# Attention block with a two-way expert layer on one core: the PV steps of a key chunk in one run of four, where they stood in two runs of two

## The reference

```
h = layernorm(x) * (1 + ca) + sa
x = x + ga * attention(h)          # 16 query heads, 4 key/value heads, head size 64, rotary, causal
h = layernorm(x) * (1 + cb) + sb
x = x + gb * experts(h)            # 8 experts (128 -> 512 -> 128, silu gate), top 2 of each token

logits = einsum('bqhgd,bkhd->bhgqk', q, k) / 8 ; masked above the diagonal
w = softmax(logits) ; out = einsum('bhgqk,bkhd->bqhgd', w, v) @ Wo + bo
```

## Time and profile before

| | |
|---|---|
| median of three runs | 1269.56 us |
| the profiled execution's own time | 1270.48 us |
| its span, first to last instruction | 1268.7 us |
| TensorE busy / VectorE busy | 86% / 67% of the span |
| ScalarE busy / GpSimd busy | 42% / 47% of the span |

### The profile page before, as it was taken

The page is one execution under the profiler, slowest core; times in us unless marked ns, Lnnn a source line. Parts: engine busy times, 40 slices in busy tenths (PEclk is TensorE's granted clock), DMA queues, the critical chain, the costliest instruction groups (busy, mean ns, idle before and its releaser), DMA issues.

```text
span 1268.7 us, 16442 instructions
## 1 busy us (share of the span) xinstructions
PE 1087.0 (86%) x5698; PEld 657.3 (52%) x5698; DVE 852.9 (67%) x1659; ACT 535.8 (42%) x1149; POOL 591.3 (47%) x639
## 2 busy tenths in 40 slices
PE   3589999999999999999999999999999840199930
PEld 2356555555555655455555555565555330199930
DVE  3657878776878786777878776878777374044422
ACT  1335544545445454544544545445444412144410
POOL 1725655634545673634645644544453336411136
PEclk9699999999999999999999999999999955599975
DMA  8000000000000000000000000000000061211112
GB/s 226 1 1 1 1 1 1 1 1 1 1 1 1 1 1 1 1 1 2 1 1 1 1 1 1 1 1 1 1 1 1 1 199 35 64 39 49 32 36 76
DMA packets 33088, 24.84 MB, mean 20 GB/s; under 512 B 8816, under 2 KB 28272, under 8 KB 33008
## 3 DMA queue, kind: packets, MB, share of 16 engines
q1 hardware_dynamic: 23664, 17.25, 4.5%
q0 software_dynamic: 2048, 4.20, 1.1%
q10 hardware_dynamic: 7296, 2.36, 0.8%
HBM read 15.54 MB, written 8.26 MB: 19 GB/s over the span
## 4 chain that ended last, share of the span: by engine, by line
PE 74%; DVE 11%; POOL 7%; issue 3%; DMA 2%; ACT 2%; ACTq 1%; POOLq 0%; DVEq 0%
PE PS L1156 19%; PE PS L1110 12%; PE PS L1138 11%; PE PS L1140 9%; PE PS L1221 4%; PE PS L1240 3%; POOL sent L586 3%; PE PS L1086 2%; PE PS L1175 2%; DVE part_max L847 2%; POOL full L600 2%; PE PS L1123 2%; PE PS L1093 2%; PE PS L1166 2%; DVE full L863 2%
## 5 line engine op out<-in xcount | busy, mean ns | idle before, releaser
L847 DVE TENSOR_REDUCE part_max<-PS 128x1 f32<-128x512 f32 (+2 forms) x576 | 340.1, 618 | 132.9 <-PE PS L1110 110.5
L656 ACT ACTIVATE full<-PS 128x512 f32<-128x512 f32 x384 | 223.4, 599 | 198.3 <-PE PS L1140 185.7
L1138 PE MATMUL PS<-rounded 128*128 128x512 f32 (+3 forms) x640 | 271.9, 425 | 5.9 <-ACT diag L665 2.4
L1110 PE MATMUL PS<-rounded 128*128 128x512 f32 (+3 forms) x640 | 250.0, 417 | 2.4 <-DVE V L828 1.3
L533 POOL TENSOR_TENSOR full<-full 128x512 f32<-128x512 f32 x128 | 164.0, 1313 | 156.2 <-PE PS L1156 155.2
L1140 PE MATMUL PS<-rounded 128*128 128x512 f32 (+3 forms) x640 | 233.3, 365 | 0.0
L665 ACT ACTIVATE diag<-PS 128x512 f32<-128x512 f32 (+3 forms) x256 | 111.3, 441 | 214.8 <-PE PS L1143 184.9
L1110 PEld LDWEIGHTS PS<-rounded 128*128 128x128 f32 x640 | 119.7, 193 | 138.2 <-DVE part_max L847 62.9
L561 POOL TENSOR_TENSOR rot_cos<-qkv_sb,cos_sb 128x320 f32<-128x320 f32 x64 | 60.4, 943 | 279.5 <-DVE qkv_sb L825 277.2
L1156 PE MATMUL PS<-full,V 128*64 128x512 f32 x768 | 190.0, 605 | 0.0
L1138 PEld LDWEIGHTS PS<-rounded 128*128 128x128 f32 x640 | 122.9, 192 | 80.8 <-ACT diag L665 27.0
(11 more groups left out here) (140 smaller groups left out, 1439.8 us busy)
## 6 DMA issues: line engine op xcount, KB each, us to landing
full<-in_L_ffn_experts_w_dram SPq DMA_DIRECT2D x16, 256.0 KB, 6.7
sent<-sum_cols SPq DMA_DIRECT2D x1, 2496.0 KB, 19.6
made<-attnT SPq DMA_DIRECT2D x39, 64.0 KB, 1.5
full<-sent SPq DMA_DIRECT2D x9, 256.0 KB, 3.0
out_dram<-XA SPq DMA_DIRECT2D x4, 256.0 KB, 2.4
wqkv<-in_L_attn_Wq_dram ACTq DMA_DIRECT2D x1, 512.0 KB, 4.3
bqkv<-in_L_attn_bq_dram ACTq DMA_DIRECT2D x1, 512.0 KB, 9.8
wo_sb<-in_L_attn_Wo_dram SPq DMA_DIRECT2D x1, 512.0 KB, 8.8
```

Of the source, the lines that this page charges most:

```text
L656: nc.scalar.activation(full[:, k % QUADS, r, :], PS[:, bank, :], ACT.Exp).then_inc(probs_ready, 1)
L847: nc.vector.reduce_max(part_max[:, t, b:b + 1], PS[:, bank, 0:width], AX.X).then_inc(ring_dve, 1)
L1110: last = nc.tensor.matmul(PS[:, bank, 0:w], QT[:, ch % 2, h, t * P:(t + 1) * P], KT[:, 0, keys:keys + w], start=True, stop=not last_bank)
L1138: nc.tensor.matmul(o, KT[:, 0, keys:keys + P], QT[:, ch % 2, h, q0:BANK], start=True, stop=False)
```

## The change

Off the diagonal the pending PV steps are now held until the scores of r = 3 are issued; before, they went out at r = 1 and r = 3. So behind the eight score steps of a key chunk come four PV steps in one run: the last one of the chunk before and tiles 0, 1 and 2. The room left on the line behind r = 0, 1 and 2 is 2.1 for each PV step that is pending by then (2.1, 4.2 and 6.3; before, 2.1 behind r = 0 and 2.1 behind r = 2), and the room of the run itself is 8.4 (before 4.2 twice). The `poolsum` of key chunk 1 in the stages with three key chunks off the diagonal moves from behind r = 1 to behind r = 3 of key chunk 2, since the PV step that it waits for is in that run. What is computed stays as it is.

```diff
             for r in range(TB):
                 main += [("s", J, q, r, 0), ("s", J, q, r, 1)]
-                if q < J // PAIRS and r % 2 == 0:
+                if q < J // PAIRS and r < TB - 1:
                     main.append(("gap", 2.1 * len(pending)))
                 else:
                     main += pending
                     pending = []
-                if r == (1 if q < J // PAIRS else 0) and q > 1:
+                if r == (TB - 1 if q < J // PAIRS else 0) and q > 1:
                     if q < CHUNKS - 1:
                         main += [("poolsum", J, m, q - 1) for m in range(2)]
                     else:
                         main += [("quadsum", J, m, part) for m in range(2) for part in range(4)]
                 pending.append(("pv", J, q, r))
```

## The result

The changed kernel takes 1292.1 us (median of 4 runs, 1291.3 to 1295.9) against 1269.4 us, a ratio of 1.0186 with a 95% interval of 1.0163 to 1.0208. The forecast was 1265.0 us, so the sign was wrong, and the time lies far above the 1275 up to which the wide range reached. The profiled execution took 1295.9 us, 3.7 above the median; its span was 1294.1.

The account below looks back on a forecast made before the run. TensorE's throughput was taken as the bound, VectorE close behind in places. Terms -17.0 + 1.4 + 2.5 + 1.2 + 4.0 + 1.2 + 1.0 + 1.2 = -4.5 us gave 1265.0; own range 1261 to 1267, 8-in-10 range 1256 to about 1275.

Parts of the forecast that it names:

- Item 1: 48 key chunks off the diagonal, one PV run fewer each at 0.355 us: 17.0 us off TensorE.
- Item 2: Score steps wait for two score banks' exponentials: +1.4 us last stage, +2.5 other stages 7, +1.2 stage 6.
- the upper bound of 0.47 a chunk: Largest score-bank loss allowed per key chunk in stage 7 of the first three groups; 0.28 was taken.
- Item 3: VectorE lacks row maxima during the longer PV run: +4.0 us in stage 5, +1.2 stage 4, +1.0 stage 3.
- rival B: VectorE starved behind the run in every dense chunk of stages 2 to 5: slower, 1278.1 us; chance 0.24.
- B's term for the ring: TensorE waits 0.8 us for the ring in each of 24 chunks of stages 2 to 5: +19.2 us.
- item 4: Side steps denser between runs bring `proj` nearer to `low`: 0.3 us per stage with four `low`, +1.2 in all.
- Item 5: Later GpSimd and `quadsum` sums cost nothing; if the margin fails, up to 2 us once at the end.

Follow-up runs that it names:

- The run alone: Kernel before with runs of four PV steps, every side step kept between the same scores (old line): 1287.9 us against 1269.4.
- short maxima: Row maxima off the first query chunk taken over 128 columns, not up to 512: kernel before 1260.7 us, runs of four on the old line 1261.0.
- the line alone: Kernel before, still runs of two and two, with scores and side steps at the changed kernel's places (new line): 1281.7 us, ratio 1.0098.
- Three ring banks: Three score and three ring banks for two and four, with 128-column maxima: 1274.9 us with runs of four (old line), 1262.3 with two and two.

## Why the prediction was wrong

**Item 1, the run's ends: right.** The run of 16 records takes 3.58 us (below), forecast 3.59, and the account gives 0.3 to 0.4 per run end against 0.355. The section Back-to-back issue gap of "TensorE: Matmul & The Clock Gate" in the Trainium skill gives the 216 ns as the gap of an isolated matmul, by its columns alone, and a shorter one, 131 ns, for a sustained stream. That the end of a run is free was my inference from it, and the runs don't bear it out; the 0.22 to 0.23 us between like score matmuls agree with its first figure, not with its second.

**Item 2, the score banks: right in the last stage, too small in stage 7 of the other groups.** The last stage's key chunk 2, changed kernel, takes 1029.49 - 1020.44 = 9.05 us, forecast 9.03, before 8.92:
```profile
1020.44 0.50 PE L1138 MATMUL PS<-rounded 128*128 128x512 f32 x1
...
1021.92 0.50 PE L1138 MATMUL PS<-rounded 128*128 128x512 f32 x1 [0.28 <-ACT full L656]
...
1023.34 0.50 PE L1138 MATMUL PS<-rounded 128*128 128x512 f32 x1 [0.20 <-ACT full L656]
...
1024.76 0.50 PE L1138 MATMUL PS<-rounded 128*128 128x512 f32 x1 [0.20 <-ACT full L656]
...
1025.91 3.65 PE L1156 MATMUL PS<-full,V 128*64 128x512 f32 x16
1029.49 0.50 PE L1138 MATMUL PS<-rounded 128*128 128x512 f32 x1
```
Stage 7 of group 1 got 1.6 us longer where I had 0.2 shorter. The run alone makes it 1.0 longer (40.9 against 39.9), and with short maxima it stays so, so this isn't VectorE's pace; even the upper bound of 0.47 a chunk gives only 0.35. The other 0.6 shows only with both together (the line alone has 39.8). Stage 6 got 0.5 us shorter, forecast 0.8.

**Item 3, VectorE's supply: the step that failed.** "Where VectorE has room this costs nothing" took the room as a mean over a chunk. The mechanism was named, and rival B put its place and kind right; the sizes came out of a sum (12.34 + 0.6 + 1.1) that lets VectorE's work of a chunk lie anywhere in it. It can't: TensorE may be ahead of VectorE by four banks only, so the work ordered in front of the run must nearly be done before the run starts. What counts is the time TensorE has in front of the run against VectorE's work there. With two and two half of the PV work was part of that time. So chunk 1 of stage 4, whose VectorE had 10% to spare, was costed at 13.7 and took 14.7 us, and chunk 1 of stage 5, costed at 13.9 to 14.0, took 14.4. In all I had 4.0 + 1.2 + 1.0 = 6.2 us for this step; by the short maxima it is 17.6, so B's term for the ring, 0.8 us in each of 24 chunks or 19.2, was about right in size. What B lacked too is the other half: it kept my items 2 and 4 at 6.3 us, and some 17 us of waits stay with VectorE relieved.

Stage 2 doesn't speak for this step. Its chunk 0, costed at nothing, took 3.6 us more with 1.5 back in chunk 1, but it also holds more side work than before (67 matmuls, before 52), and runs of two on the new line lose the same 2.1 us in this stage.

**The line was not costed.** I read off it that side steps move off the diagonal, and counted them as VectorE's load. That it also puts steps nearer to what they wait for was only item 4, at 1.2 us for the whole kernel. Beside runs of two it is 11.6 us, about 6 of them with VectorE relieved, beside runs of four 4.2, and the one place that I followed is exactly item 4's chain, `proj` to `low`, with `qk` behind it. How the rest divides wasn't followed.

**Item 5, the sums: right in the whole, off at the end.** Moving the poolsum costs nothing (1269.9 us against 1270.2). GpSimd's five additions in stage 6 are now done at 506.69 + 6.21 = 512.9 and no VectorE wait for them appears. At the very end `quadsum` takes 5.99 us in place of 4.91, 1.1 us once, and not because a sum came too late: GpSimd's fifth addition ends at 1027.08 + 6.70 = 1033.78, and the second head is due some 2.4 us behind 1031.94, at 1034.3. VectorE's second addition, while GpSimd's fifth runs, takes 1.78 us instead of 0.68, and the fifth itself 1.77 instead of 1.27. Additions of 1.7 us, while the other engine adds too, were no term of mine.
```profile
506.69 6.21 POOL L533 TENSOR_TENSOR full<-full 128x512 f32<-128x512 f32 x5 [8.57 <-PE PS L1156]
```
```profile
1031.94 5.99 DVE L863 TENSOR_TENSOR full<-full 128x512 f32<-128x512 f32 x8 [15.07 <-PE PS L1156]
```
```profile
1027.08 6.70 POOL L533 TENSOR_TENSOR full<-full 128x512 f32<-128x512 f32 x5 [4.45 <-PE PS L1156]
```

What stays open: with VectorE relieved, 14.6 us of waits (twice 7.3) still take the place of the 17 saved. By place 3 of the 7.3 are before L1110, 2.3 before the two score matmuls, the rest before `rowsum` and `qmax`. None of these places was tested by itself. Three ring banks show that depth matters; more than four weren't tried, since scores, ring and the two PV banks take all eight.

## What to carry to other kernels

A long block of one kind of work on the engine that bounds is also time in which the others catch up. Before merging two blocks, compare what the neighbour must do in front of the merged block with the time that is left in front of it, at the depth of the buffers between them; the mean load of the whole stretch doesn't show this. And a change in the weights by which a planner places steps is a change of its own: try it without the other.

## What the runs showed of the hardware

A stretch at the lower clock can follow a short wait. In the runs of four with short maxima on the new line, right behind the wait of 1.85 us before 350.45, TensorE's granted clock is 0.50, its lower level of 1.2 GHz, in one stretch, and 1.00 and 0.99 around it (columns: us, busy and count of PE, PEld, DVE, ACT, POOL; clock; DMA share; GB/s):
```profile
347.50:351.00 3.50, 1.65 (x14) 1.31 (x13) 1.29 (x5) 1.96 (x6) 1.27 (x2) 1.00 0.00 0
351.10:354.50 3.40, 3.40 (x9) 1.33 (x10) 0.58 (x2) 1.40 (x3) 0.00 (x0) 0.50 0.00 0
354.50:358.00 3.50, 3.50 (x24) 1.90 (x22) 1.97 (x4) 1.26 (x3) 0.00 (x0) 0.99 0.00 0
```
```profile
352.40 0.63 PE L1140 MATMUL PS<-rounded 128*128 128x512 f32 x1
352.83 0.33 PE L1143 MATMUL PS<-causal,ident 128*128 128x128 bf16 x1
```
At that level a matmul of 512 columns holds the next one's start for 0.43 us, not 0.23 (L1140 at 352.40, L1143 at 352.83), so such a stretch costs 1.5 to 1.7 us. The trace of that kernel has six of them in the attention (one in each of the four groups at this place), that of the runs of four on the old line with short maxima one. Five more at this price are some 8 us, as much as the 6.9 us by which the new line is slower there. That they are its cause wasn't tested: the profiled execution, at 1270.7 us and a granted clock of 0.930, is the slowest of the ten, while others at 0.935 and 0.936 took 1266.5 and 1268.0, and two and two on the same line lose 6.1 us with one such stretch.
